# Seven block products for eight: pairs of token tiles through Strassen's scheme in a folded adaLN-FFN kernel

## The reference

```python
# first layer, x is 2048 x 1024
base   = x @ W.T
logits = x @ Wr.T + 5 * one_hot(language)          # 8 experts
gates  = softmax over the top two of logits, 0 elsewhere
h      = x @ A.T                                   # 8 experts x 16
y      = base + 2 * (h * gates) @ B
# second layer
gates2 = softmax(y @ Wr2.T)                        # 4 experts
proj   = y @ A2.T                                  # 4 experts x 8
out    = x + y @ W2.T + b + 2 * (proj * gates2) @ Bm
```

## Time and profile before

| | |
|---|---|
| median of three runs | 363.53 us (363.41 to 363.54) |
| span of the profiled execution | 360.5 us |
| TensorE busy in the span | 354.0 us, 98%, 2038 matmuls |
| VectorE busy | 118.3 us, 33% |
| ScalarE busy | 78.6 us, 22% |
| fold stage ends, token tiles begin | 113.17 us |
| one token tile | 15.2 us |
| moved by DMA | 26.90 MB |

### The profile page before, as it was taken

One profiled execution on the slowest core, in us unless ns is written; L12 is line 12 of the kernel. 1 busy time (PEld: TensorE's weight loads), 2 busy tenths in 40 slices (PEclk: granted clock), 3 DMA queues, 4 the chain that ended last, 5 costly groups with the idle time before them and its releaser, 6 DMA issues.

```text
span 360.5 us, 5416 instructions
## 1 busy us (share of the span) xinstructions
PE 354.0 (98%) x2038; PEld 348.1 (97%) x2038; DVE 118.3 (33%) x364; ACT 78.6 (22%) x182; POOL 1.3 (0%) x11
## 2 busy tenths in 40 slices
PE   8999999999999999999999999999999999999995
PEld 6998999999999999999999999999999999999995
DVE  3557412220221424233242332423234232342321
ACT  5536202220222121121212212122121220212101
POOL 1000000000000000000000000000000000000000
PEclk9999999999999999999999999999999999999999
DMA  7853111101110030311303123030230303201011
GB/s 281 266 200 135 58 58 58 39 19 58 58 59 5 0 116 0 116 61 55 116 0 116 47 70 116 0 116 21 95 116 0 116 0 116 105 11 58 0 58 61
DMA packets 7319, 26.90 MB, mean 75 GB/s; under 512 B 942, under 2 KB 942, under 8 KB 7312
## 3 DMA queue, kind: packets, MB, share of 16 engines
q1 hardware_dynamic: 7168, 26.80, 21.3%
q10 hardware_dynamic: 144, 0.01, 0.0%
HBM read 18.42 MB, written 8.39 MB: 74 GB/s over the span
## 4 chain that ended last, share of the span: by engine, by line
PE 90%; DMA 5%; DVE 2%; ACT 1%; issue 0%; SPq 0%; DVEq 0%
PE sums L499 89%; DMA stage<-head 4%; DMA stage<-fold_tail 1%; DVE m_low L349 1%; ACT m_high L255 1%; DVE st_low L349 1%; DVE c_low L349 1%; ACT st_high L255 1%; PE turned L610 0%; PE turned L600 0%; DVE rows L487 0%; SPq L188 0%; DVEq L486 0%
## 5 line engine op out<-in xcount | busy, mean ns | idle before, releaser
L499 PE MATMUL sums<-c_low,st_high 128*128 128x384 f32 (+1 forms) x384 | 112.7, 347 | 0.0
L499 PE MATMUL sums<-c_high,st_high 128*128 128x384 f32 (+1 forms) x384 | 111.1, 343 | 0.0
L499 PE MATMUL sums<-c_high,st_low 128*128 128x384 f32 (+1 forms) x384 | 111.0, 343 | 0.0
L499 PEld LDWEIGHTS sums<-c_high,st_low 128*128 128x128 f32 x384 | 70.6, 188 | 0.9
L499 PEld LDWEIGHTS sums<-c_high,st_high 128*128 128x128 f32 x384 | 70.1, 188 | 1.0
L499 PEld LDWEIGHTS sums<-c_low,st_high 128*128 128x128 f32 x384 | 69.5, 188 | 1.3
L499 PE MATMUL sums<-m_high,st_high 128*128 128x384 f32 (+1 forms) x216 | 47.2, 330 | 0.9 <-DVE c_low L349 0.8
L499 PE MATMUL sums<-m_low,st_high 128*128 128x384 f32 (+1 forms) x216 | 46.1, 327 | 0.0
L499 PE MATMUL sums<-m_high,st_low 128*128 128x384 f32 (+1 forms) x216 | 45.9, 325 | 0.0
L499 PEld LDWEIGHTS sums<-m_high,st_high 128*128 128x128 f32 x216 | 36.1, 192 | 1.9 <-DVE c_low L349 1.6
L349 DVE TENSOR_TENSOR st_low<-stage,st_high 128x1024 fp32r<-128x1024 f32 (+1 forms) x31 | 31.6, 1019 | 16.9 <-ACT m_high L255 10.1
(11 more groups left out here) (58 smaller groups left out, 181.7 us busy)
## 6 DMA issues: line engine op xcount, KB each, us to landing
stage<-tokens SPq DMA_DIRECT2D x16, 512.0 KB, 3.8
out<-rows SPq DMA_DIRECT2D x16, 512.0 KB, 2.8
stage<-head SPq DMA_DIRECT2D x7, 658.0 KB, 4.5
stage<-fold_tail SPq DMA_DIRECT2D x7, 512.0 KB, 3.5
stage<-gate_proj SPq DMA_DIRECT2D x1, 544.0 KB
stage<-mix_rows SPq DMA_DIRECT2D x1, 392.0 KB
stage<-head SPq DMA_DIRECT2D x1, 384.0 KB, 3.3
stage<-head SPq DMA_DIRECT2D x1, 274.0 KB, 2.8
```

The lines of the kernel that those rows point to most:

```text
L499: return nc.tensor.matmul(out_, lhs, rhs, start=start, stop=stop, skip_group_check=True)
```

## The change

The 16 tiles become 8 pairs. For a pair the wide product is that of a 2 x 2 block matrix (tile 0 and 1, first and second half of the 1024 inputs) with a 2 x 2 block matrix of C (first and second half of the inputs, columns 0 to 383 and 384 to 767). It is made by seven products of blocks instead of eight. With x blocks X11, X12 (tile 0), X21, X22 (tile 1) and C blocks B11, B12, B21, B22:

- S1 = X21 + X22, S2 = S1 - X11, S3 = X11 - X21, S4 = X12 - S2 (VectorE, for each pair, `add_s`);
- T1 = B12 - B11, T2 = B22 - T1, T3 = B22 - B12, T4 = B21 - T2 with one sign turned (VectorE, once, in `fold_out`);
- the products P1 = X11 B11, P6 = S2 T2, P2 = X12 B21, P7 = S3 T3, P5 = S1 T1, P4 = X22 T4, P3 = S4 B22, in this order on TensorE, each of 4 x 3 matmuls of 384 columns into one bank.

Partial sums leave their bank between products: ScalarE copies P1 to `rows`, VectorE adds what lies in the bank to it and stores it in `rows`, and the last product of a bank is added at the end. S and T are split in high and low parts as everything else. The narrow products of both tiles stand at the head of the pair, and the gate chain is made for both tiles together: where the instruction can take both, one, else two in a row. The first pair is written out before the loop, since T is rounded and split there.

```diff
-        c_high = sb("c_high", [P, 1 + KC, COLS], F32R)
-        c_low = sb("c_low", [P, 1 + KC, COLS], F32R)
+        c0_high = sb("c0_high", [P, MCOLS], F32R)
+        c0_low = sb("c0_low", [P, MCOLS], F32R)
+        ct_high = sb("ct_high", [P, KC, TAIL], F32R)
+        ct_low = sb("ct_low", [P, KC, TAIL], F32R)
+        cw_high = sb("cw_high", [P, 3, HALF, WIDE], F32R)
+        cw_low = sb("cw_low", [P, 3, HALF, WIDE], F32R)
+        s_plain = sb("s_plain", [P, 4, HALF, P])
+        t_high = sb("t_high", [P, 4, HALF, WIDE], F32R)
+        t_low = sb("t_low", [P, 4, HALF, WIDE], F32R)
+        s_high = sb("s_high", [P, 4, HALF, P], F32R)
+        s_low = sb("s_low", [P, 4, HALF, P], F32R)
...
+            def store(j):
+                sp.wait_ge(tails_out, j + 1)
+                sp.wait_ge(a_out, j + 1)
+                sp.wait_ge(c_out, j + 1)
+                sp.dma_start(out[bass.ds(2 * j * P, P), :], rows[:, 0, :]).then_inc(stored[0], 16)
+                sp.wait_ge(b_out, j + 1)
+                sp.wait_ge(d_out, j + 1)
+                sp.dma_start(out[bass.ds((2 * j + 1) * P, P), :], rows[:, 1, :]).then_inc(stored[1], 16)
...
-            def token_tile(t, j, odd):
-                par = TPAR[odd]
-                slot = SLOT[par]
...
-                wide_parts(range(0, TURN_AT))
-                pe.wait_ge(u_ready, t + 1)
-                nc.tensor.transpose(ut_psum, u[:, :], ident[:, :]).then_inc(u_turned, 1)
...
-                wide_parts(range(LORA_AT, 3 * KC)).then_inc(contracted, 1)
-                pe.wait_ge(v_ready, t + 1)
-                nc.tensor.transpose(vt_psum, v_rows[:, :], ident[:, :]).then_inc(v_turned, 1)
-                for lhs, rhs in parts:
-                    for p in (0, 1):
-                        mm(piece(par, p, 0, WIDE), lhs[:, :], rhs[:, 0, p * WIDE:(p + 1) * WIDE])
-                pe.wait_ge(vt_ready, t + 1)
-                for p, a, b in ((0, 0, WIDE), (2, 2 * WIDE, D), (1, WIDE, 2 * WIDE)):
-                    mm(piece(par, p, 0, b - a), vt[:, :], mix[:, a:b]).then_inc(z_ready, 1)
+            def wide(n, a_high, a_low, a_at, b_high, b_low, b_at, fresh):
+                for k in range(HALF):
+                    for kind in (HH, HL, LH):
+                        lhs = (a_high, a_high, a_low)[kind]
+                        rhs = (b_high, b_low, b_high)[kind]
+                        last = mm(bank(n), lhs[:, a_at[0], a_at[1] + k, :], rhs[:, b_at, k, :],
+                                  start=fresh and k == 0 and kind == HH, stop=k == HALF - 1 and kind == LH)
+                return last
...
+            def pair(j, first=False):
+                if not first:
+                    pe.wait_ge(tails_out, j)
+                pe.wait_ge(x_split[0], j + 1)
+                tail(0, first)
+                pe.wait_ge(x_split[1], j + 1)
+                tail(1, False).then_inc(narrow_ready, 1)
+                if not first:
+                    pe.wait_ge(a_out, j)
+                of_x(BANK_A, 0, 0, B11, True).then_inc(p1_done, 1)
+                if first:
+                    pe.wait_ge(read_out[0], 3 * (2 + FOLDS // 2))
+                if first:
+                    pe.wait_ge(t_split, T2 + 1)
+                pe.wait_ge(s_split, 4 * j + S2 + 1)
+                if not first:
+                    pe.wait_ge(b_out, j)
+                wide(BANK_B, s_high, s_low, (S2, 0), t_high, t_low, T2, True).then_inc(p6_done, 1)
+                pe.wait_ge(u_ready, j + 1)
+                for t in range(2):
+                    last = nc.tensor.transpose(ut_psum[:, t, :], u[:, t, :], ident[:, :])
+                last.then_inc(u_turned, 1)
+                pe.wait_ge(r1_read, j + 1)
+                of_x(BANK_A, 0, 1, B21, False).then_inc(p2_done, 1)
+                pe.wait_ge(ut_low_ready, j + 1)
+                for t in range(2):
+                    last = lora(BANK_T + t, t, 2 * WIDE, MCOLS)
+                last.then_inc(y_small_ready, 1)
+                if first:
+                    pe.wait_ge(t_split, T3 + 1)
+                pe.wait_ge(s_split, 4 * j + S3 + 1)
+                pe.wait_ge(u2_read, j + 1)
+                wide(BANK_B, s_high, s_low, (S3, 0), t_high, t_low, T3, False).then_inc(p7_done, 1)
+                lora(BANK_A, 0, 0, WIDE)
+                if first:
+                    pe.wait_ge(t_split, T1 + 1)
+                pe.wait_ge(s_split, 4 * j + S1 + 1)
+                if not first:
+                    pe.wait_ge(c_out, j)
+                wide(BANK_C, s_high, s_low, (S1, 0), t_high, t_low, T1, True).then_inc(p5_done, 1)
+                if not first:
+                    pe.wait_ge(d_out, j)
+                lora(BANK_D, 1, WIDE, 2 * WIDE, fresh=True)
+                pe.wait_ge(v_ready, j + 1)
+                for t in range(2):
+                    last = nc.tensor.transpose(vt_psum[:, t, :], v_rows[:, t, :], ident[:, :])
+                last.then_inc(v_turned, 1)
+                if first:
+                    pe.wait_ge(t_split, T4 + 1)
+                pe.wait_ge(u3_read, j + 1)
+                wide(BANK_B, st_high, st_low, (X_SLOT[1], HALF), t_high, t_low, T4, False).then_inc(p4_done, 1)
+                pe.wait_ge(vt_ready, j + 1)
+                for t in range(2):
+                    last = mixed(BANK_T + t, t, 2 * WIDE, D)
+                last.then_inc(tails_done, 1)
+                lora(BANK_B, 1, 0, WIDE)
+                pe.wait_ge(s_split, 4 * j + S4 + 1)
+                pe.wait_ge(r22_read, j + 1)
+                wide(BANK_C, s_high, s_low, (S4, 0), cw_high, cw_low, B22, False).then_inc(p3_done, 1)
+                lora(BANK_C, 0, WIDE, 2 * WIDE)
+                mixed(BANK_A, 0, 0, WIDE).then_inc(a_done, 1)
+                mixed(BANK_D, 1, WIDE, 2 * WIDE).then_inc(d_done, 1)
+                mixed(BANK_B, 1, 0, WIDE).then_inc(b_done, 1)
+                mixed(BANK_C, 0, WIDE, 2 * WIDE).then_inc(c_done, 1)
...
+            def pair(j, first=False, last=False):
+                for n in (S2, S3, S1, S4):
+                    if first:
...
+                    round_s(j, n)
+                act.wait_ge(top_ready, j + 1)
+                for t in range(2):
+                    ins = nc.scalar.activation(pair_exp[:, t:t + 1], top[:, t, 0:1], ACT.Exp, bias=top[:, t, 1:2],
+                                               scale=-1.0)
+                ins.then_inc(pair_exp_ready, 1)
...
+                act.wait_ge(p1_done, j + 1)
+                copy(rows[:, 1, 0:WIDE], bank(BANK_A)).then_inc(r1_read, 1)
+                act.wait_ge(u_turned, j + 1)
+                copy(ut_high[:, :, :], ut_psum).then_inc(ut_high_ready, 1)
...
+                low_part(cw_low[:, B21, i, :], piece(par, 0, 0, WIDE), cw_high[:, B21, i, :])\
+                    .then_inc(read_out[par], 1)
+                dve.wait_ge(fold_high, 3 * s + 3)
+                low_part(cw_low[:, B22, i, :], piece(par, 1, 0, WIDE), cw_high[:, B22, i, :])
+                minus(t_plain[:, T2, i, :], piece(par, 1, 0, WIDE), t_plain[:, T1, i, :]).then_inc(t2_made, 1)
+                minus(t_plain[:, T3, i, :], piece(par, 1, 0, WIDE), t_plain[:, T3, i, :]).then_inc(read_out[par], 1)
+                dve.wait_ge(t2_made, i + 1)
+                minus(t_plain[:, T4, i, :], t_plain[:, T4, i, :], t_plain[:, T2, i, :]).then_inc(t4_made, 1)
...
+                nc.vector.tensor_tensor(s_of(S1), block_of(1, 0), block_of(1, 1), ALU.add).then_inc(s1_made, 1)
+                dve.wait_ge(s1_made, j + 1)
+                minus(s_of(S2), s_of(S1), block_of(0, 0)).then_inc(s_made, 1)
+                minus(s_of(S3), block_of(0, 0), block_of(1, 0)).then_inc(s_made, 2)
+                dve.wait_ge(s_made, 4 * j + 1)
+                minus(s_of(S4), block_of(0, 1), s_of(S2)).then_inc(s_made, 1)
...
+                for n in (S2, S3, S1):
+                    if first:
+                        split_t(n)
+                    split_s(j, n)
+                if not first:
+                    split_s(j, S4)
+                dve.wait_ge(narrow_ready, j + 1)
+                link(nc.vector.tensor_tensor(logits[:, :, :], both(LOGIT_AT, LOGIT_AT + E1),
+                                             lang_bias[:, bass.ds(2 * j, 2), :], ALU.add))
+                dve.sem_inc(carried, 1)
+                nc.vector.max(top[:, 0, :], logits[:, 0, :])
+                link(nc.vector.max(top[:, 1, :], logits[:, 1, :]))
+                nc.vector.max_index(top_at[:, 0, :], top[:, 0, :], logits[:, 0, :])
+                nc.vector.max_index(top_at[:, 1, :], top[:, 1, :], logits[:, 1, :]).then_inc(top_ready, 1)
...
+                nc.vector.reciprocal(pair_scale[:, :], pair_half[:, :])
+                nc.vector.tensor_scalar(gate_second[:, 0, :], expert_no[:, :], top_at_f[:, 0, 1:2],
+                                        pair_exp[:, 0:1], ALU.is_equal, ALU.mult)
+                link(nc.vector.tensor_scalar(gate_second[:, 1, :], expert_no[:, :], top_at_f[:, 1, 1:2],
```

(63 more changed lines are left out.)

471 lines of the change are left out of this document (273 added, 198 removed).

## The result

| | before | after |
|---|---|---|
| time, median of the runs, us | 363.53 (363.41 to 364.05, 4 runs) | 350.87 (348.79 to 351.24, 4 runs) |
| profiled execution, its own time, us | 363.5 | 351.24 |
| span of that execution, us | 360.5 | 348.9 |
| matmuls | 2038 | 1942 |

The changed kernel takes 0.965 of the time before (95% interval 0.962 to 0.968): faster by 12.7 us. The forecast was 351.1.

The account below looks back on a forecast made before the run. TensorE, busy for 98% of the span, was taken as the bound. Terms of -16.8 + 1.5 + 0.8 + 2.1 = -12.4 us gave a span of 348.1; with 3.0 above it, 351.1 us, range 348.6 to 355.0.

Parts of the forecast that it names:

- (1): Wide products on TensorE: 12 fewer matmuls per pair over 8 pairs, 96 x 0.175 = 16.8 us less.
- (2): Gate chain in the loop: doubled instructions add 1.02 us, still hidden under wide matmuls with 0.16 spare; cost nothing.
- (3): Second chain (maximum, exponential, v): about 2.4 us, under 5.25 us of matmuls; cost nothing.
- (4): New VectorE additions and sums after the second chain: 4.8 us, ready 1.1 us before the last block product; cost nothing.
- (5): Seam between fold and tokens, once: TensorE loses 1.5 us before u's transposes and 0.8 us before the 292-column products.
- (6): Kernel end: additions after the last matmuls 0.58 us later, two tiles stored together 1.50 more; 2.1 us lost.
- The sum: All terms together: -16.8 + 1.5 + 0.8 + 2.1 = -12.4 us.
- A: Rival: doubled gate-chain instructions cost their whole duration, so u's transposes wait 0.38 us in each pair; 354.3 us; 18%.
- B: Rival: VectorE's sums are late and the last block product waits, 0.1 to 1.4 us per pair; 7%.
- C: Rival: ends faster, as seam waits shrink or stores land sooner; 347.6, more likely 349 to 350 us; 10%.
- D: Rival: matmuls with their own stationary matrix in one bank start farther apart; slower than before, up to 366.7 us; 4%.

Follow-up runs that it names:

- bank-by-bank run: Kernel before, with a tile's 48 wide matmuls going to one bank until its 24 are done, then to the other: 363.34 us, 0.999 of the time before.
- six more: The changed kernel run again, unchanged: 350.89 us, 0.963 of the time before.
- reordered kernel: Changed kernel with T1, S1, T4 and S4 split later on VectorE in the first pair only: 348.67 us, 0.959 of the time before.
- reordered kernel with pieces: Changed kernel with the first pair's splits reordered, mix products in another order and the last pair stored in six pieces: 345.91 us, 0.953 of the time before.
- late sum: Changed kernel with two unread 1024-column additions on VectorE ahead of the S sums in the six middle pairs: 358.38 us, 0.989 of the time before.
- eighth product: Changed kernel with S3 x T3 computed once more in each pair: 369.32 us, 1.016 of the time before.

## Why the prediction was right

- **(1) Products, 16.8.** 96 matmuls at 0.174, shown by putting them back (16.6). Stationary matrices of their own and a single bank cost nothing, as costed; the bank-by-bank run gives 0.999.
- **(2) Gate chain, 0.16 spare: right in its length, too small in its margin.** Forecast 3.52 us long, it took 3.49 in the first pair and 3.50 later. The neighbours started 0.08 (maximum) and 0.15 (gates) apart, as costed. The 0.04 and 0.17 for the semaphore and for loading u are not seen: the transposes start 0.05 to 0.06 after u, and 0.3 were spare. It changed nothing in the loop, where no wait came. The Trainium skill's page "VectorE: DVE Perf Modes" (section "Side-by-side: where the cycles go for N=2048 bf16") gives some 158 cycles of fixed cost, from which 0.1 of wait per pair had been estimated if none of it hid behind a neighbour; the trace shows part of it hidden, and no wait.
- **(3) Second chain.** 2.24 us (218.47 to 220.71) for a forecast of 2.4, with time to spare.
- **(4) Sums.** The last addition ends 14.4 after the pair's first wide matmul (210.95 to 225.33) against 14.6, and the block product starts 15.6 after it against 15.7. 1.0 to 1.1 are spare against 1.1.
- **(5) Seam.** 1.27 and 0.7 lost against 1.5 and 0.8. The three T and S splits took until 11.4 after the first narrow matmul, forecast 11.3 (a T takes ScalarE 1.49, where the prediction's own two lengths also give 1.49 and it wrote 1.46; VectorE is the slower, so nothing hangs on it). The transposes started 14.9 after it, forecast 15.07, and the 0.2 are the load of u, which is not seen here either.
- **(6) End.** 5.7 us behind the last matmul against 5.9. The additions end 1.25 after it, as forecast (1.24); the two stores together cost 1.3 more than one did, against 1.50.
- **The sum.** The token stage and what follows it fell by 14.8 less 1.9, that is 12.9, against 12.4 forecast. The span fell by only 11.6, since the head of this execution was 1.35 longer.
- **Outside the span: two errors that cancel.** The prediction added 3.0 us to the span, as the median of the runs before had it over the profiled span of 360.5. But most executions of either kernel lie some 2 above their span, and before's profiled one had a quick head: 11 other runs of it have spans of 360.6 to 362.3, 361.5 in the median, and 23 more have 359.5 to 363.4 with a median of 361.6. From 361.5, 12.4 less is 349.1, and the spans of the changed kernel are 346.9 to 349.1 in its four runs, 347.1 to 349.4 in the six more. So the sum was right, and the base it stood on was a span 1.0 too small with 1.0 too much around it. That this came out even is luck: the span of one execution is no base for a forecast to a microsecond.

The rivals: A had more room than it was given (0.3 us for 0.16), B as much (1.0 to 1.1 for 1.1), and neither occurred. C did not happen, but the reordered kernel gets what C described by design. D is refuted.

## What to carry to other kernels

When TensorE is the bound, an algorithm that leaves out products is worth their number times the distance between their starts (here 96 x 0.174 us), as long as every other engine still ends its chain before TensorE needs the result. That has to be worked out for each chain. Then test the margins: take away six matmuls of cover, or add two additions, and see whether the wait comes at the size that the margin says. Work that is done once, at the seam of two stages, is cheapest to mend by the order of one engine's list: ask of each item when it is first needed. And look at the last store, since nothing hides it: here six pieces in place of two whole tiles, with the mix products reordered, took 1.6 us off the end.

## What was not expected of the hardware

- The narrow products began at 112.80, 113.02, 113.08, 113.17, 114.40, 114.50, 114.52, 114.92, 115.31 and 116.66 in ten profiled executions. Seven of them, from 112.80 to 116.66, are of the changed kernel and its variants, in which TensorE has the same work up to there. Up to 3.9 us of a difference between two profiles can be the head. The ten fall into two groups by the rounding of the second block of x, which waits for its load: it starts at 6.24 to 6.61 in the four that begin the token stage by 113.17, and at 7.63 to 8.62 in the other six.
- The latest, 116.66, has a second cause, the granted clock of TensorE. In the reordered kernel with pieces it was 0.84, 0.50 and 0.81 in the stretches 32 to 34, 34 to 36 and 36 to 38 us, where 0.50 is the lower of the two levels, 1.2 GHz; TensorE had been busy for 0.99 of the 2 us before. From the first matmul after that pause to the token stage it took 84.5 us (from 32.16), where the reordered kernel without pieces took 82.95 (31.55 to 114.50): 1.55 for the clock, which was back at 1.00 from 38 us on. In the execution of the changed kernel TensorE was busy for 0.86 of the same 2 us and the clock stayed at 1.00, so what set it off is not shown.
- A second independent small instruction on VectorE starts 0.08 to 0.18 us behind the first, though each lasts 0.15 to 0.28 us.
- The transposes that wait for u start 0.05 to 0.06 us after it, with no sign of the 0.17 that had been charged for loading it; the block product that waits for the late sum starts 0.15 after it.
- The time above the span: 1.7 to 3.0 in all kernels but one, and 3.6 to 5.5 in the four runs with the eighth product; unexplained.
